# Three plain cross-attentions of a fused four-layer kernel: their pipeline, scores and masks rearranged, and one addition moved in the latent attention

## What is computed

```python
# L0, L2: 16 heads of 8; L3: 8 heads of 64 (no biases)
q = heads(layernorm(x) @ Wq + bq) * D ** -0.5
k, v = heads(ctx @ Wk + bk), heads(ctx @ Wv + bv)
score = einsum('bhqd,bhkd->bhqk', q, k)
# L2: score + mask[b, 0, q, k] * -1e9      L3: where(mask[b, k], score, -inf)
x = x + (softmax(score) @ v) @ Wo + bo
```

## Time and profile before

| | us |
|---|---|
| median of three runs | 2007.45 (2007.34, 2007.45, 2012.43) |
| the profiled execution | 2016.02, its span 2014.3 |
| TensorE busy | 1817.5 (90%) |
| VectorE busy | 1520.5 (75%) |
| ScalarE busy | 1007.3 (50%) |
| GpSimd busy | 786.9 (39%) |

### The profile page before, as it was taken

How to read it: one execution, slowest core, us unless ns; L and a number is a source line. 1 busy time by engine, 2 the same in 40 slices (tenths; PEclk the granted TensorE clock), 3 DMA queues, 4 the chain that set the end, 5 groups by cost and what they waited for, 6 DMA issues and landing times. The chain is left out here.

```text
span 2014.3 us, 29655 instructions
## 1 busy us (share of the span) xinstructions
PE 1817.5 (90%) x10579; PEld 1223.9 (61%) x10579; DVE 1520.5 (75%) x2730; ACT 1007.3 (50%) x1492; POOL 786.9 (39%) x640
## 2 busy tenths in 40 slices
PE   4988999679999999999998999879789999979798
PEld 2556888444444444444445777645457789957676
DVE  6677996767677767676757888799799965567698
ACT  2555888445666566656644555435400120045586
POOL 2332331156777676766662344233202402012131
PEclk8997999779999999999997999889989999989799
DMA  1001211100000000000000212000000010000032
GB/s 64 1 0 26 105 64 53 50 0 1 1 1 1 1 1 1 1 1 1 1 1 19 85 63 84 12 1 0 17 11 26 32 53 0 0 12 0 6 127 95
DMA packets 21179, 51.27 MB, mean 25 GB/s; under 512 B 3563, under 2 KB 11383, under 8 KB 18116
## 3 DMA queue, kind: packets, MB, share of 16 engines
q1 hardware_dynamic: 20596, 49.53, 7.2%
q10 hardware_dynamic: 464, 0.20, 0.0%
HBM read 48.48 MB, written 1.25 MB: 25 GB/s over the span
## 5 line engine op out<-in xcount | busy, mean ns | idle before, releaser
L1513 POOL TENSOR_TENSOR sb_L_total<-sb_L_total,sb_L_probT 128x512 f32<-128x512 f32 (+1 forms) x192 | 267.1, 1415 | 50.5 <-ACT sb_L_probT L1817 46.6
L395 POOL TENSOR_TENSOR sb_L_prob<-sb_L_prob,sb_L_rsum 128x616 f32<-128x616 f32 (+1 forms) x96 | 98.1, 1043 | 270.0 <-DVE sb_L_rsum L637 270.0
L1817 ACT ACTIVATE sb_L_probT<-banks 128x1024 f32<-128x1024 f32 x128 | 131.1, 1025 | 139.0 <-PE banks L1646 138.6
L1874 DVE TENSOR_REDUCE sb_L_top_tok<-banks 128x2 f32<-128x1024 f32 x128 | 155.9, 1220 | 25.7 <-PE banks L1613 25.7
L1656 PE MATMUL banks<-sb_L_probT,sb_L_v 128*64 128x512 f32 x512 | 138.2, 619 | 0.2 <-DVE sb_L_mixedT L1925 0.2
L1510 POOL TENSOR_TENSOR sb_L_total<-sb_L_probT 128x512 f32<-128x512 f32 x64 | 80.7, 1281 | 131.0 <-ACT sb_L_probT L1817 131.0
L543 ACT ACTIVATE sb_L_probT<-banks 77x512 f32<-77x512 f32 x160 | 89.7, 589 | 76.9 <-PE banks L446 76.9
L2238 DVE SCALAR_TENSOR_TENSOR sb_L2f_hid<-banks,sb_L2f_weight,sb_L2f_hid 128x512 f32<-128x512 f32 x176 | 122.5, 744 | 2.5 <-PE banks L97 1.6
L2308 DVE SCALAR_TENSOR_TENSOR sb_resid<-banks,sb_L2f_weight,sb_resid 128x128 f32<-128x128 f32 x192 | 67.1, 351 | 62.5 <-PE banks L97 57.9
L1218 DVE TENSOR_TENSOR sb_L0f_hid_low<-sb_L0f_raw,sb_L0f_hid_high 128x1024 fp32r<-128x1024 f32 x64 | 88.7, 1401 | 29.4 <-ACT sb_L0f_hid_high L1176 29.0
L432 PE MATMUL banks<-sb_L_kdiag,sb_L_qT 128*128 (+2 forms) x192 | 84.9, 584 | 21.2 <-DVE sb_L_prob L628 10.1
(11 more groups left out here) (411 smaller groups left out, 5227.3 us busy)
## 6 DMA issues: line engine op xcount, KB each, us to landing
sb_L0f_wide<-spread_L0f SPq DMA_DIRECT2D x7, 1024.0 KB, 5.8
sb_L1f_wide<-spread_L1f SPq DMA_DIRECT2D x7, 1024.0 KB, 7.5
sb_L3f_wide<-spread_L3f SPq DMA_DIRECT2D x7, 1024.0 KB, 5.4
sb_fetched<-L2f_w SPq DMA_DIRECT2D x12, 256.0 KB, 2.6
sb_fetched<-L1f_gu SPq DMA_DIRECT2D x8, 336.0 KB, 3.0
sb_fetched<-L0f_w SPq DMA_DIRECT2D x8, 259.0 KB, 2.7
sb_fetched<-L0f_w SPq DMA_DIRECT2D x8, 256.0 KB, 3.5
sb_normT<-L2f_w SPq DMA_DIRECT2D x2, 768.0 KB, 5.5
```

The source lines that it names most:

```text
L395: pool.tensor_tensor(grid, grid, bcast(rsum[:, i % PROBS, half], [None, KEYS]), ALU.mult).then_inc(normed, 1)
L1513: pool.tensor_tensor(sums[rows], sums[rows], probT[rows, k, h], ALU.add).then_inc(added[h], 1)
L1817: act.activation(probT[:, k], ps[:, slot:slot + 2, :], ACT.Exp).then_inc(exped, 1)
L1874: dve.tensor_reduce(top_tok[:, :, k:k + 1].rearrange("p h k -> p (h k)"), ps[:, banks:banks + 2, :], AX.X, ALU.max).then_inc(bound_read, 1)
```

## The change

In the plain attentions:

- the loops over batches are written out, and scores go three tiles ahead instead of four; VectorE does `shift(n + 2)`, `add(n - 1)`, `add_up(n + 1)` in tile n; key spreads of batches 1 to 3 move into tiles 0, 3 and 6; `v_now` and its copies go; `qT` has two buffers;
- for 16 heads the scores are split: keys and queries get high and low parts in fp32r (ScalarE rounds, VectorE takes the keys' low part, GpSimd spreads it in `low_keys` and takes the queries' low part in `low_queries`), the scores lie in four banks of 308 columns, with three fp32r matmuls each; they stand ahead of the third product instead of behind the fourth, and ScalarE's exponential ahead of the third copy;
- in L2 ScalarE scales all masks once; in odd tiles the mask (high and low part) is added by TensorE, a unit matrix times the mask, eight matmuls more; in even tiles VectorE adds it as before;
- GpSimd adds the output bias in two halves.

In the latent attention VectorE's `add_result` moves ahead of `low_queries`. The core of the diff:

```diff
+        AHEAD, SCORES_AT = 3, GROUPS - 2 if split else GROUPS
@@ scores
+                        for g in range(BANKS):
+                            last = split_product(pe, ps[:, g, 0:H // BANKS * KEYS], (q_high[:, b % HALVES, t:t + P], q_low[:, b % HALVES, t:t + P]),
+                                                 (high[:, g], low[:, g]), stop=not masked_on_pe(n))
+                        if masked_on_pe(n):
...
+                            for x in (mask_high, mask_low):
+                                for g in range(BANKS):
+                                    last = pe.matmul(ps[:, g, 0:H // BANKS * KEYS], eye[:], x[:, n // 2, :], start=False, stop=x is mask_low)
@@ TensorE, tile
-                    for g in range(1, GROUPS):
-                        if g + 1 < GROUPS:
-                            turn(n, i, g + 1)
-                        product(n, b, i, g)
-                    if more:
-                        scores(n + TPB, b + 1, i)
+                    for g in range(GROUPS):
+                        if g > 0 and g + 1 < GROUPS:
+                            turn(n, g + 1)
+                        if g == SCORES_AT and later(n, AHEAD):
+                            scores(n + AHEAD)
+                        product(n, g)
+                        next_queries()
+                    if SCORES_AT == GROUPS and later(n, AHEAD):
+                        scores(n + AHEAD)
                     output(n)
@@ TensorE, start
-                for n in range(TPB):
-                    scores(n, 0, n)
+                for n in range(AHEAD):
+                    scores(n)
@@ ScalarE
+                    act.activation(kT_high[:], kT[:], ACT.Copy).then_inc(k_high_ready, 1)
+                    if on_pe:
+                        fetch.wait(act, "mask")
+                        act.activation(mask_raw[:], masks, ACT.Copy, scale=-1e9).then_inc(mask_scaled, 1)
@@ GpSimd
+                for n in range(TILES):
+                    if split and n % TPB == 2 and n // TPB + 1 < BATCH:
+                        low_queries(n // TPB + 1)
+                    divide(n)
+                    if masked_on_pe(n + 3):
+                        low_mask(n + 3)
+                    if split and n in (3, 6):
+                        low_keys(n // 3 + 1)
@@ VectorE, tile
-                    if later(n, 3):
-                        shift(n + 3, b + (i + 3) // TPB, i + 3, base)
                     if later(n, 2):
-                        add_up(n + 2, i + 2, base)
-                    add(n)
-                    if i == TPB - 1 and later(n, 1):
-                        place_v(b + 1)
+                        shift(n + 2)
+                    if n > 0:
+                        add(n - 1)
+                    if later(n, 1):
+                        add_up(n + 1)
+                    if n in (0, 3, 6):
+                        spread_keys(n // 3 + 1)
@@ latent attention, VectorE
+                    if turn == 1:
+                        dve.wait_ge(bias_added, 1)
+                    if turn > 0:
+                        add_result(turn - 1)
                     if much:
                         low_queries(turn + 2)
```

More of the change, by code:

```diff
@@ L331, in cross_attention, with masked_on_pe @@
     PROBS = TPB
-    biased = FB == 1
+    biased = split = FB == 1
+    on_pe = split and mask == "scaled"
+    def masked_on_pe(n):
+        return on_pe and n < TILES and n % 2 == 1
     with ExitStack() as ctx:
@@ L354, in cross_attention, with masks_added @@
             "summed", "normed", "turned", "turn_read", "pv_done", "mixed_ready", "y_done", "y_added"))
[L355 to L362, removed]
+        def masks_added(n):
+            return sum(not masked_on_pe(m) for m in range(n))
+        PV, Y, Q = (6, 7, (6, 6)) if split else (5, 6, (7, 4))
+        if split:
+            K_AT, V_AT, TURN = (0,), Y, 4
+            BANKS = 4
+            heads = ps[:, 0:BANKS, 0:H // BANKS * KEYS].rearrange("p g (h k) -> p g h k", h=H // BANKS)
         else:
@@ L420, in queries, with wait_scores_read @@
                         pe.wait_ge(q_ready, b * FB + j - 1)
-                    pe.matmul(ps[:, Q[j % 2], :], wq[:, j * P:(j + 1) * P], c.normT[:, bass.ds(b * SEQ, SEQ)], start=True, stop=True).then_inc(q_done, 1)
-                def scores(n, b, i):
+                    pe.matmul(ps[:, Q[j % 2], :], wq[:, j * P:(j + 1) * P], c.normT[:, b * SEQ:(b + 1) * SEQ], start=True, stop=True).then_inc(q_done, 1)
+                def wait_scores_read(n):
+                    if mask is None or masked_on_pe(n):
+                        pe.wait_ge(shifted, n + 1)
+                    else:
+                        pe.wait_ge(masked, masks_added(n) + 1)
@@ L424, in scores @@
+                def scores(n):
+                    b, i = n // TPB, n % TPB
+                    if i == 0 and split:
+                        pe.wait_ge(kdiag_low_ready, b + 1)
+                        pe.wait_ge(q_low_ready, b + 1)
+                    elif i == 0:
+                        pe.wait_ge(q_ready, b * FB + FB)
                     if i == 0:
-                        pe.wait_ge(q_ready, b * FB + FB)
-                    if later(n, -1):
-                        pe.wait_ge(score_read, n)
+                        pe.wait_ge(kdiag_ready, (b + 1) * FB)
+                    if n > 0:
+                        wait_scores_read(n - 1)
@@ L686, in _ @@
                         nxt.norm.normalise(dve, 1)
+                add(TILES - 1)
                 dve.wait_ge(y_added, TILES + 1)
```

252 lines of the change are left out of this document (139 added, 113 removed).

## The result

The changed kernel takes 1978.62 us in the median of four runs (1971.47 to 1982.05), the kernel before beside it 2008.32. The ratio is 0.9844, with a 95% interval of 0.9811 to 0.9876: 25 to 38 us faster, 31 by the ratio. The forecast was 19 us, counted from a median of 2007.45, with a range of 1978 to 2000; the ratio applied to that median gives 1976, just under the range. The profiled executions, spans of 1974.7 and 2014.3 us, lie 39.6 us apart. So two traces alone tell a stage to a few us at best.

What follows compares the result with a forecast made beforehand. TensorE and VectorE are both near their limit in L2; TensorE paces the latent stage. L0 -6.5, L2 +1.2, L3 -5.0, latent -9.0 sum to -19.3 us: 1996.7 from 2016.0 profiled, 1988 on the 2007.45 median; range 1978 to 2000.

Steps and rivals of the forecast that it cites:

- the starts: Plain stages before their main parts: key spreads and a scores round leave the path; L0 -6.3, L2 -6.8, L3 -4.7 us.
- the port: SBUF port shared by VectorE and GpSimd at the starts: 1 us cost in L0, 0.5 in L2, bounds 0 and 3.
- my 2.5 us: L0's and L2's starts: first scores come 2.5 us later, waiting for low keys and queries; between 2 and 3.5.
- the scored tile: Steady 16-head tile with scores: tile without scores less an idle plus split scores, 6.54 us, 0.14 under the old.
- rival (c): L0 and L2 scores: alternating fp32r matmuls need weight loads; at 0.25 us each, 21 us slower, 2028.6; chance 0.07.
- L2's main part: Main part of L2: odd tiles 7.76 us with masks on TensorE, even 6.54; +8.3, counted as +8.0 us.
- a few tenths: L2's main part: dropping the copies of v_now takes back a few tenths of a us.
- pays nothing: L2's main part: VectorE losing a 1.44 us pass in half the tiles gains nothing, since TensorE is later.
- the latent edit: Latent turns: adding the result before the low queries removes TensorE's 22 waits, 11.1 us; -9.0 us, bounds 0 and 11.1.
- rival (a): Latent turns: the removed wait is taken over by the next one, nothing gained there; total -10.3, 1997 us; chance 0.17.
- L3: Third plain attention, 8 heads: start -4.7, query waits -0.8, extra scored tile and low clock +0.5; -5.0 us.
- Rival (d): Starts lose nothing to port or clock, L0 and L2 end stalls shrink, latent gains all 11: about -28, 1979; chance 0.11.

Runs made afterwards that it cites:

- the experiment with the scores behind: Changed kernel with the split scores moved back behind the last product: ratio 0.9844 to the kernel before, no difference from the changed kernel.
- the trace with the output late: Changed kernel with a 16-head tile's output product moved behind the next tile's first turn: ratio 0.979 to the kernel before.

## Why the prediction was wrong

**Right: direction and mechanism of the starts; their sum in part by luck.** Forecast in sum -17.8 us before the main parts (L0 -6.3, L2 -6.8, L3 -4.7), measured -17.9, with L0 1.1 us better and L3 1.4 worse. The first scores of L0 stood at 27.94 (28.1), the main part at 42.85 (43.4). That the spreads left the path is shown by putting them back. In L2 I had 20 us from first scores to main part at most, it took 17.5 (1285.50 to 1302.98). The luck is inside L0's start: its first scores took 3.5 us until VectorE could begin (27.94 to 31.40, matmuls 0.26 us apart) where I had 1.8. Against that stood 1 us that I had set aside for the port and that the chain behind them did not lose, and third scores at full pace (41.04 to 42.85, 1.8 us), where I had 1.8 to 3.6. The port did cost something ahead of them: the first low keys took GpSimd 3.40 us beside VectorE's key spread, 2.28 later, and this lay inside my 2.5 us. In the kernels below L0's start ends 21.9 to 24.1 us after it began, as more or fewer of its scores run at the slow pace.

**Wrong: the scored tile, the term that failed.** "5.08 - 0.33 + 1.79 = 6.54" was 6.25, in 26 tiles of L0 and L2, 7.5 us of the 13 that the plain stages gained beyond their forecast. The step was a sum of durations with one idle taken off: it left out that a block put between two others also takes away the seams between those. The rows of before could have told me. By the same rule the old tile is 5.08 - 0.40 + 2.17 = 6.85 us, and the earlier trace rows has 6.68; 0.17 of seams, as in the experiment with the scores behind. A rule that misses a known case by 0.17 us doesn't carry a term of 0.14 us, nor the claim that the new tile is "only 0.14 us under the old one". The size of an fp32r matmul, the rival (c) that would have made it slower, held: the twelve start 0.14 us apart at full clock (83.67, 83.81 and 83.96 in the trace with the output late), and 0.26 at the low clock (1287.15 and 1287.41 at L2's start in after; granted 0.50 from 1287 to 1289).

**Wrong: L2's main part.** +8.0 forecast, +2.2 measured. Of the 5.8 us between them 3.8 are the same 0.29 in 13 tiles; the masks at 1.11 instead of 1.22 make 0.8 in seven tiles; the rest, 1.2, fits the stalls at the copies of v_now, of which I had counted "a few tenths", but was not measured alone. In before TensorE waits 0.96 us for the last copy at 1419.82, and the two tiles from there on, which carry no scores, take 5.69 and 6.03 us; in after such tiles take 5.09 and 5.08. That the pass taken off VectorE in half of the tiles "pays nothing" did not hold with tiles of 6.25 us in place of 6.54: without the relief L2 is 3.2 us longer.

**Half right: the latent edit.** The 11.1 us of waits went, as said. That VectorE's next copy is "not later" was wrong: the low queries, moved behind the addition, take up to 1.82 us instead of 1.17 beside GpSimd, and in 12 to 20 of 32 turns TensorE waits for the key squares. The cause is shown: with the low queries elsewhere these waits are gone and the kernel is 7 us faster. I had the mechanism (the shared port of VectorE and GpSimd) and put it only where the change adds work, not where it moves a step into GpSimd's way. The timed gain, 2.4 to 7.2 us, is under my 9.0, and by it rival (a), that the wait is taken over by a next one, was true for about half; in the total this hid part of what the tile gained. The mean of the traces' turns, 8.7 us shorter, is near my 9.0, and why the two differ stays open.

**L3.** Forecast -5.0, measured -6.2: less in the start (-3.3) and more in the main part (-2.9), where the first output comes 6.9 us after the start and not 8.9, and the two later tiles with queries take 7.8 us and not 8.2. Of this I had named the shorter tiles alone, and for the queries' wait. Some of it has other causes: before begins this main part at half the clock (granted 0.50 from 1795 to 1798), after at full clock, and with its loops written out the kernel before has 8.0 in those two tiles.

**Rival (d)**, 1979, was nearest, and partly for another reason than it gave: not the port at the starts but the tile.

**Still open:** the timed gain of the plain stages is 23 to 29 us, the three stages' differences make 23. What is over lies within the noise of both and in stages without an edit, whose times and clock differ between traces of one and the same code. Which of it the change causes by moving those stages, no run here separates.

## What to carry to other kernels

Before a tile's new length is worked out as "old parts less an idle plus the new block", work out the old tile by the same rule: the miss is the size of the seams, and it is the accuracy of everything that follows. When a step of VectorE is moved, look at what GpSimd does at the new place as much as at what VectorE does; a two-operand step in SBUF belongs into an idle behind which nobody waits. And a wait that takes the place of the one removed is cured at the engine that is late, not by asking later. A stage's gain is to be read from several traces or from timed runs of the edit alone.

## What the runs showed of the hardware

One and the same VectorE instruction, a subtraction of 512 columns between SBUF tiles, took 0.68, 1.17, 1.32, 1.55 or 1.82 us, by what GpSimd did beside it. When both engines began within 0.03 us of each other, either of the two was the longer one, and the other kept its time. A subtraction of 1232 columns took 1.44 in most tiles and 1.63, 1.83, 2.08 or 2.57 in a few; with the scores read from PSUM it kept 1.44, 24 times of 24 in after. The Trainium skill, page "SBUF — State Buffer", section "SBUF: two separate sides", has only the shared port pair of the two engines in contention; the rows agree, since the form that reads PSUM did not grow.

The latent turns come in two lengths for the same turn (19.7 or 20.4 us, 19.2 or 19.8), and how many of each differs between seven kernels whose latent code is the same: 642 to 652 us for the 32 turns. Two traces of the kernel before, one and the same code, have 659.4 and 652.9. A gain of 5 us in such a stage can't be read from two traces.
